# Another order for the opening of a three-stage transformer kernel: loads, weight products, first values and keys

## The reference, cut to what matters

```python
x_in = _ln(ctx, lnkv_g, lnkv_b)
k = x_in @ wk + bk
v = x_in @ wv + bv
slots = q_mu + jnp.exp(q_logsig) * noise          # noise = layernorm(x)
for _ in range(3):
    prev = slots
    q = _ln(slots, lnq_g, lnq_b) @ wq + bq
    attn = softmax(einsum('bnd,bkd->bnk', k, q) / scale) + EPS; attn = attn / sum
    slots = (attn^T @ v) @ wu + bu + prev
    h = _ln(slots, lnm_g, lnm_b) @ w1 + b1
    slots = gelu(h) @ w2 + b2 + slots
    slots = _ln(slots + x_cls, lnp_g, lnp_b)
x = x + slots
x = x + layernorm(gelu(_ln(x) @ tern(W_fc))) @ tern(W_proj)
```

## Time and profile before

| | us |
|---|---|
| median of 3 runs (lowest, highest) | 335.87 (335.57, 335.93) |
| the profiled execution, its own time | 337.69 |
| its span in the trace | 335.6 |
| PE busy, share of the span | 316.7 (94%) |
| DVE busy | 277.8 (83%) |
| ACT busy | 228.0 (68%) |
| POOL busy | 214.2 (64%) |

### The profile page before, as it was taken

One profiled execution on the slowest core, in us unless ns is written; L12 is line 12 of the kernel. 1 busy time (PEld: TensorE's weight loads), 2 busy tenths in 40 slices (PEclk: granted clock), 3 DMA queues, 4 the chain that ended last, 5 costly groups with the idle time before them and its releaser, 6 DMA issues. The chain is left out here.

```text
span 335.6 us, 6157 instructions
## 1 busy us (share of the span) xinstructions
PE 316.7 (94%) x1758; PEld 261.8 (78%) x1758; DVE 277.8 (83%) x816; ACT 228.0 (68%) x504; POOL 214.2 (64%) x417
## 2 busy tenths in 40 slices
PE   8999999999999999999998998999894989999995
PEld 8888887888888888888887777887671767777774
DVE  2799967989899999999998999887678388888763
ACT  2368985967667878587599474865566386777871
POOL 3169866265679755666987646678766856566331
PEclk9999999999999999999999999999999699999999
DMA  7989000000000000000000000000000000000001
GB/s 283 314 281 401 11 1 0 0 2 0 1 3 0 1 3 0 2 2 0 2 0 0 3 0 2 3 0 2 0 0 0 3 32 33 32 31 2 32 33 63
DMA packets 5312, 13.24 MB, mean 39 GB/s; under 512 B 672, under 2 KB 672, under 8 KB 4896
## 3 DMA queue, kind: packets, MB, share of 16 engines
q1 hardware_dynamic: 4160, 10.88, 9.0%
q10 hardware_dynamic: 1120, 1.98, 1.6%
HBM read 10.76 MB, written 2.10 MB: 38 GB/s over the span
## 5 line engine op out<-in xcount | busy, mean ns | idle before, releaser
L285 DVE BATCH_NORM_STATS2 stats<-S 128x6 f32<-128x256 f32 x112 | 42.1, 417 | 9.1 <-DMA S<-ctx 3.6
L336 PE MATMUL ps_mid<-XT,KT 128*128 128x256 f32 x192 | 46.0, 383 | 3.4 <-ACT XT L352 3.4
L336 PE MATMUL ps_low<-V,PR 128*128 128x257 f32 x192 | 46.1, 382 | 0.9 <-DVE PR L877 0.6
L336 PE MATMUL ps_mid<-XT,wt 128*128 128x256 f32 x192 | 45.6, 380 | 0.8 <-ACT XT L352 0.7
L336 PE MATMUL ps_low<-wn,GT 128*128 128x256 f32 x192 | 45.4, 379 | 0.0
L336 PEld LDWEIGHTS ps_low<-V,PR 128*128 128x128 f32 x192 | 36.1, 190 | 7.4 <-DVE PR L877 2.5
L336 PEld LDWEIGHTS ps_mid<-XT,KT 128*128 128x128 f32 x192 | 34.6, 190 | 8.5 <-ACT XT L352 4.8
L336 PEld LDWEIGHTS ps_low<-wn,GT 128*128 128x128 f32 x192 | 36.2, 190 | 4.9
L303 POOL TENSOR_TENSOR lnm_ab<-lnm_mv,mhalf 128x2 f32<-128x2 f32 x24 | 17.3, 721 | 35.7 <-DVE lnm_mv L293 35.7
L336 PEld LDWEIGHTS ps_mid<-XT,wt 128*128 128x128 f32 x192 | 34.7, 190 | 5.1 <-ACT XT L352 1.2
L352 ACT ACTIVATE XT<-ps_t 128x512 f32<-128x512 f32 x56 | 33.0, 590 | 8.2 <-PE ps_t L328 8.2
(11 more groups left out here) (127 smaller groups left out, 708.9 us busy)
## 6 DMA issues: line engine op xcount, KB each, us to landing
S<-ctx SPq DMA_DIRECT2D x8, 256.0 KB, 3.9
X<-x SPq DMA_DIRECT2D x8, 256.0 KB, 4.0
out<-X SPq DMA_DIRECT2D x8, 256.0 KB, 2.0
rowv<-rows SPq DMA_DIRECT2D x1, 1920.0 KB, 9.9
wf<-w_fc_t SPq DMA_DIRECT2D x1, 1024.0 KB, 11.9
wf<-w_proj_t SPq DMA_DIRECT2D x1, 1024.0 KB, 13.6
wt<-w_tr ACTq DMA_DIRECT2D x1, 512.0 KB, 4.2
wn<-w_nat ACTq DMA_DIRECT2D x1, 512.0 KB, 5.5
```

The source lines that it names most:

```text
L285: dve.bn_stats(ln.st[:, at, j, 0:6], tiles[:, j]).then_inc(ln.stats_done, 1)
L336: last = pe.matmul(dst(m), lhs_t[:, c, m * P:(m + 1) * P], rhs[:, c, 0:n], start=(c == 0), stop=(c == 1))
```

## The change

- The transposed weights wk and wq, one load on the ACT queue so far, become two loads of 256 KB: wk stays first on ACT, wq goes first on SP, ahead of S[0] and S[1]. Both count on `wkq_in`, whose waits go to 32.
- SP then waits for `wkq_in` instead of for wk before it issues X[0].
- On ACT the order becomes wk transposed, `colv`, wv transposed, wu, then wk with wv in one load, then the early rows. In all the same bytes.
- TensorE makes 6 warm-up products instead of 11, then both weight products, then the transpose of item 0, `column` of wk, values of item 0, `column` of wv, keys of item 0, `column` of wq with `ckv`, the transpose of item 1 and the product of `bcol` with wu. Step 0 of TensorE's loop becomes empty.
- DVE scales Wkq ahead of the moments of S[1], takes the moments of X[0] (`rows_x`) before it waits for the `column` of wv, and makes both halves of `ckv` behind that wait. Its loop is unchanged.
- ACT copies the transpose of item 0 before it waits for the early rows and takes their exponential.

```diff
 LEAD = 7
-WARM_UP = 11
+WARM_UP = 6
 SUM_STEP = 5
...
     act.activation(XT[:, u].rearrange("p c k -> p (c k)"), ps_t[u][:], ACT.Copy).then_inc(t_copied, 1)
-        FOLD_CK, FOLD_CV, FOLD_K, FOLD_V, FOLD_ALL = 3, 8, 10, 12, 15
+        FOLD_W, FOLD_C, FOLD_K, FOLD_V, FOLD_ALL = 6, 8, 10, 12, 15
         TERN_ALL = (ROUNDS - 1) * B
...
         sp.dma_start(flat(dst, b), src[b]).then_inc(s[b % 2], 16)
+    sp.dma_start(wt[:, TQ].rearrange("p c d -> p (c d)"), w_tr[1]).then_inc(wkq_in, 16)
     load(S, c_v, ctx_in_sem, 0)
     load(S, c_v, ctx_in_sem, 1)
-    sp.wait_ge(wk_in, 16)
+    sp.wait_ge(wkq_in, 32)
     for b in range(B):
...
         act.dma_start(dst, src).then_inc(s, 16)
-    load(wt[:, TK:TQ + 1].rearrange("p w c d -> p w (c d)"), w_tr[0:2].rearrange("w p n -> p w n"), wkq_in)
+    load(wt[:, TK].rearrange("p c d -> p (c d)"), w_tr[0], wkq_in)
     load(colv[:], cols, cols_in)
-    load(wn[:, WK].rearrange("p c d -> p (c d)"), w_nat[0], wk_in)
-    load(wn[:, WV:WU + 1].rearrange("p w c d -> p w (c d)"), w_nat[1:3].rearrange("w p n -> p w n"), wvu_in)
     load(wt[:, TV].rearrange("p c d -> p (c d)"), w_tr[2], wvu_in)
+    load(wn[:, WU].rearrange("p c d -> p (c d)"), w_nat[2], wvu_in)
+    load(wn[:, WK:WV + 1].rearrange("p w c d -> p w (c d)"), w_nat[0:2].rearrange("w p n -> p w n"), wk_in)
     load(rowv[:, 0:ROWS_EARLY], rows[0:ROWS_EARLY].rearrange("(a n) -> a n", a=1)
...
     ln_apply(act, lnc, 0, 0, S[:, 0], XR[:, 0], xc_ready)
+    copy_xt(act, 0, 0)
     act.wait_ge(bu_in, 16)
     act.activation(row("q_logsig"), row("q_logsig"), ACT.Exp).then_inc(sig_ready, 1)
-    copy_xt(act, 0, 0)
     ln_apply(act, lnc, 1, 1, S[:, 1], XR[:, 1], xc_ready)
...
         bn_rows(dve, lni, u, Y[:, b])
-    for b in range(2):
-        rows_c(b, b)
-        bn_sum(dve, lnc, b, b)
+    rows_c(0, 0)
+    bn_sum(dve, lnc, 0, 0)
     dve.wait_ge(cols_in, 16)
+    for c in range(C2):
+        dve.tensor_scalar(kgain[:, c:c + 1], col("lnq_g", c), LOGIT_SCALE, None, ALU.mult).then_inc(w_fold, 1)
     dve.wait_ge(w_prod, 1)
...
                           ALU.mult).then_inc(w_fold, 1)
+    rows_c(1, 1)
+    bn_sum(dve, lnc, 1, 1)
     dve.wait_ge(w_prod, 2)
-    dve.tensor_tensor(ckv[:, 0:2, 0], ps_low[0][:, 0, 0:2], colv[:, COL["bk"]:COL["bk"] + 2],
-                      ALU.add).then_inc(w_fold, 1)
-    for c in range(C2):
-        dve.tensor_scalar(kgain[:, c:c + 1], col("lnq_g", c), LOGIT_SCALE, None, ALU.mult).then_inc(w_fold, 1)
-    dve.wait_ge(w_prod, 3)
     for c in range(C2):
...
                           ALU.mult).then_inc(w_fold, 1)
+    rows_x(0, 0)
     dve.wait_ge(w_prod, 4)
-    dve.tensor_tensor(ckv[:, 2:4, 0], ps_low[0][:, 1, 0:2], colv[:, COL["bv"]:COL["bv"] + 2],
+    dve.tensor_tensor(ckv[:, 0:2, 0], ps_low[0][:, 1, 0:2], colv[:, COL["bk"]:COL["bk"] + 2],
                       ALU.add).then_inc(w_fold, 1)
-    dve.wait_ge(w_fold, FOLD_CV)
+    dve.tensor_tensor(ckv[:, 2:4, 0], ps_low[0][:, 1, 2:4], colv[:, COL["bv"]:COL["bv"] + 2],
+                      ALU.add).then_inc(w_fold, 1)
+    bn_sum(dve, lnx, 0, 0)
+    dve.wait_ge(w_fold, FOLD_C)
     dve.wait_ge(consts, 5)
...
                           ALU.mult, ALU.mult).then_inc(w_fold, 1)
-    rows_x(0, 0)
-    bn_sum(dve, lnx, 0, 0)
     dve.wait_ge(bu_in, 16)
...
         pe.matmul(ps_t[1][:, 0:P], ones[:], ones[:], start=True, stop=True)
-    pe.wait_ge(wkq_in, 16)
+    pe.wait_ge(wkq_in, 32)
     product(pe, side(ps_mid[0]), wt[:, TK], wt[:, TQ]).then_inc(w_prod, 1)
+    pe.wait_ge(wvu_in, 32)
+    product(pe, side(ps_mid[1]), wt[:, TV], wn[:, WU]).then_inc(w_prod, 1)
+    def values(b, u):
+        pe.wait_ge(t_copied, b + (1 + RING))
+        pe.wait_ge(low_read, 2 * b + 2)
+        product(pe, side(ps_low[u][:, 0]), XT[:, u], Wvu).then_inc(low_ready, 1)
+    def keys(b, u):
+        pe.wait_ge(mid_read, 2 * b + 2)
+        product(pe, side(ps_mid[u]), Wkq, XT[:, u]).then_inc(mid_ready, 1)
+    pe.wait_ge(consts, 5)
+    context_t(0, 0)
     pe.wait_ge(cols_in, 16)
     pe.wait_ge(wk_in, 16)
-    column(ps_low[0][:, 0], wn[:, WK], lambda c: col("lnkv_b", c)).then_inc(w_prod, 1)
-    pe.wait_ge(wvu_in, 32)
-    product(pe, side(ps_mid[1]), wt[:, TV], wn[:, WU]).then_inc(w_prod, 1)
-    column(ps_low[0][:, 1], wn[:, WV], lambda c: col("lnkv_b", c)).then_inc(w_prod, 1)
-    pe.wait_ge(consts, 5)
-    context_t(0, 0)
-    pe.wait_ge(w_fold, FOLD_CK)
+    column(ps_low[0][:, 1, 0:2], wn[:, WK], lambda c: col("lnkv_b", c)).then_inc(w_prod, 1)
+    pe.wait_ge(w_fold, FOLD_W)
+    values(0, 0)
+    column(ps_low[0][:, 1, 2:4], wn[:, WV], lambda c: col("lnkv_b", c)).then_inc(w_prod, 1)
+    keys(0, 0)
+    pe.wait_ge(w_fold, FOLD_C)
     column(ps_low[1][:, 0], wt[:, TQ], lambda c: ckv[:, c]).then_inc(w_prod, 1)
+    context_t(1, 1)
     pe.wait_ge(cv_spread, 2)
...
     last.then_inc(w_prod, 1)
-    def keys_values(b, u):
-        pe.wait_ge(t_copied, b + (1 + RING))
-        if isinstance(b, int) and b == 0:
-            pe.wait_ge(w_fold, FOLD_V)
-        pe.wait_ge(low_read, 2 * b + 2)
-        product(pe, side(ps_low[u][:, 0]), XT[:, u], Wvu).then_inc(low_ready, 1)
-        pe.wait_ge(mid_read, 2 * b + 2)
-        product(pe, side(ps_mid[u]), Wkq, XT[:, u]).then_inc(mid_ready, 1)
     def prologue(b, u, first, last):
+        if b == 0:
+            return
         if last is None or last < B - 1:
             context_t(b + 1, 1 - u)
-        keys_values(b, u)
+        if b == 1:
+            pe.wait_ge(w_fold, FOLD_K)
+        values(b, u)
+        keys(b, u)
     pairs(prologue)
```

## The result

The changed kernel takes 340.97 us (median, 340.16 to 341.77) against 335.90 us of the kernel before in the same comparison: ratio 1.0152, 95% interval 1.0117 to 1.0186. Forecast were 339.2 us and a range of 338.0 to 341.2; the sign and the range held, the size was 3.3 us forecast and 5.1 measured. Medians in this document are over all executions, while ratios leave out those that took over 1.5% more than the fastest of the same kernel, which were two of ten of the kernel with the bias products first (341.3 and 341.6 us, without a trace, mean clock 0.98).

The account below looks back on a forecast made before the run. DVE was taken to pace the opening loop, its start setting the end. That start moves from 14.86 to 18.2 us, so 335.87 + 3.3 = 339.2 us; own range 338.1 to 340.0, stated range 338.0 to 341.2.

Parts of the forecast that it names:

- The loop hangs on DVE's start, and everything behind passes it on: Opening loop: DVE paces it at 4.15 us a step, and its later start reaches the end one for one.
- Rival A: Opening loop: TensorE, not DVE, paces it and is free 1.4 us earlier for item 2's transpose: 334.5 us; chance 0.09.
- The order costs 3.3 us: Opening: values 0 and keys 0, 3.52 us, precede the `bcol` product; DVE's loop starts at 18.2 instead of 14.86.
- The loads: Opening queues: first weights at 4.1 us, S[0] at 5.94 (5.1 to 5.3 by bytes), wk with wv at 8.4 to 9.7.
- rival B: Opening: wk with wv lands at 11, so the run starts at 11.2, 1.2 us more: 340.4 us; chance 0.12.
- The clock, "no cost": TensorE's weight products: clock still rises at about 6 us despite a 0.2 us gap at 3.9; no cost.
- rival C: Opening: TensorE stays at 1.2 GHz through the second weight product, run from 11.6, 1.6 us more: 340.8 us; chance 0.10.
- The work done ahead buys idle time.: TensorE's loop: early values and keys give nothing back; it idles from about 17.4 to item 2's transpose at 22.0.
- No row shows how few warm-ups are enough: Warm-up: the rows agree on two clock levels but leave open how many products release the higher one; no size given.

Follow-up runs that it names:

- the kernel with the bias products first: Changed kernel with `column` of wv and wq, transpose of item 1 and `bcol` product put ahead of values 0 and keys 0: 336.88 us, ratio 1.0026.
- the trace with the early rise: Changed kernel with 18 products of ones filling TensorE's idle stretch before the transpose of item 2: 339.17 us, ratio 1.0112.

## Why the prediction was right in sign and too small

- *The loop hangs on DVE's start, and everything behind passes it on.* Right. The step is 4.16 us from 29.14 on, TensorE waits 4.59 us for the scaled context of item 2 (3.8 us behind the loop start, as worked out: 23.95 - 20.14 = 3.81), and the rounds begin later by the loop start's 5.28 and the 1.29 us of the slow second step. That the rounds take nothing back is nearly so: 6.56 us at their start are 6.31 at the last layer's. Rival A, TensorE's head start, fell with the same row: the head start became idle time.
- *The order costs 3.3 us.* Right: 3.2 us at the end without clock effects, the loop start at 18.32 against 18.2. As said there, the closeness is in part chance; by the other traces without the late rise it lies between 3.0 and 3.9 us at the loop start.
- *The loads.* The sizes were a little off. The first weights let the product start at 4.8 (forecast 4.1, bound 4.9 from the kernel before), which made the gap behind the warm-ups 0.76 us instead of 0.2. S[0] was in at 5.44 (forecast 5.94, by bytes 5.1 to 5.3), so bytes were the better guide in this and seven more traces (5.24 to 5.44), not in the ninth (5.80). In the trace with the early rise the context was ready at 8.9 and the run began at 9.48, not 9.99. wk never held TensorE, so rival B fell. (The 1304 KB of the prediction add up to 1292; nothing hangs on it.)
- *The clock, "no cost".* This is the step that failed, twice. The rise at about 6 us was read off a kernel whose TensorE had worked without a gap until 6; I carried it over to one with a gap of 0.76 us at 4 us and fewer products. In the profiled execution it came at about 10.8 and the run began at 11.73, 1.74 us behind the forecast and 2.25 behind the trace with the early rise. That is the start that rival C had (11.6), which had a chance of 0.10. C's time, 340.8 us, is near the median partly by luck: it left out the second fall, which costs 1.3 us, and the shorter low stretch at the last layer, which gave 2.1 back. And the stated range held because it took C in; 340.97 lies outside the forecast's own 338.1 to 340.0. The late rise came in some executions and not in others: with six warm-ups the rise came before 4.7 (one trace), at 8.3 (one), at 9.2 (two) or at 10.8 (one), with eleven between about 4 and 6.6 in all eight traces (six with the changed order or loads, two of the kernel before). The warm-ups bought certainty, and the change sold it.
- *"The work done ahead buys idle time."* The idle time was foreseen at 4.6 us, from about 17.4 to 22.0, and priced at nothing. It cost 1.3 us, because the clock is at the lower level behind it (from 24.4 on, 0.45 us after TensorE resumed). The row that prices it stood in the trace of the kernel before, at 255 to 266 us: 4.01 us of idle time, then 0.50. I weighed the wrong row, the 0.64 us before 15.05. A mechanism was named for the opening, and not asked for at the one place where the change itself made a long gap.
- *No row shows how few warm-ups are enough.* In every trace the warm-ups began with weight loads of 333 ns, the lower level, and the rise came later. The rule of the Trainium skill (TensorE: Matmul & The Clock Gate, "Part 1: The HAM clock gate") that the throttled level is the default and activity releases it agrees with that. Its remark that the moment of the rise varies from run to run, for which it gives 0.5 us to either side, holds in kind but not in size: it was before 4.7 to 10.8 us with the same opening of six warm-ups, and the measurement decides.

Sum of the profiled execution at the start of the rounds: 3.34 (order and loads, forecast) + 2.25 (clock in the weight products: run from 11.73 instead of 9.48) - 0.51 (9.48 instead of the forecast 9.99) + 0.20 (the run, 8.41 instead of 8.21) + 1.29 (clock behind the idle stretch) = 6.57; measured 6.56. The rounds then took 0.25 us off, and the last layer's entry about 2.1 by a shorter low stretch.

## What to carry to other kernels

Moving work ahead helps only if the engine that paces the next stage starts sooner; put what that start waits for (here four small bias products) first, and the large products that nobody awaits behind it. When a change opens a gap of some microseconds on TensorE, look in the trace for a gap of that length and read the clock behind it, before calling the gap free. And where TensorE must wait that long anyway, products into a free PSUM tile can pay: 2.3 us of 336 here, and most of the scatter.

## What the runs showed of the hardware

- The clock column reads 1.00 in the opening even where durations double (337 ns a weight load, products of 3.78 us instead of 1.97). From the first fall that it shows on, it agreed with the durations in the traces read here. In an opening, go by the weight loads.
- The time of the first rise differed by 6 us between executions of the same opening with six warm-ups (the first product at the upper level from 4.74 on in one, the second at the lower level until about 10.8 in another), and by 2.6 us with eleven (4.0 to 6.6, by the weight loads).
- Idle stretches of 4.0 and 4.6 us on TensorE were followed by work at 1.2 GHz in every trace that had them unfilled, for a few microseconds that differed from trace to trace (5.8 and 3.5 us in the two shown). Filled ones never were. An idle stretch of 1.1 us, in the run with the bias products first, had none behind it.
- A low clock, from 12.6, 13.4 and 14.2 us, followed three narrow `column` products in a row and a wait of 0.32 us in three traces and not in a fourth. What tells them apart stays open.
